# ScalarE sets one bank of a group's first maxima aside; VectorE takes its maximum later

## The chip, the cores and the metric

The kernel runs on one core of a Trainium2 chip. The metric is the device time of one launch in microseconds (us), taken as the median over runs. The core has five engines that work beside each other, each through its own queue in order: TensorE (PE in the profile, with its weight loads as PEld), VectorE (DVE), ScalarE (ACT), GpSimd (POOL) and SyncE (SP), which here only issues DMA transfers. Matmul results land in eight accumulation banks (PSUM), each 128 partitions by 512 fp32 numbers; all other tiles lie in on-chip memory (SBUF). Engines wait for each other on semaphores only.

## The reference

One pre-norm decoder layer on x of shape (2, 2048, 512) in fp32. The change touches its first part, self-attention with 16 heads of 64 and a relative-position bias:

```python
x = x + _L0_attn_ref(_layernorm(x), Wq, Wk, Wv, Wo, rel_bias)
    # q, k, v = proj(Wq), proj(Wk), proj(Wv)
    # scores = einsum('bhqd,bhkd->bhqk', q, k) + bias[buckets]
    # attn   = softmax(scores, axis=-1)
    # ctx    = einsum('bhqk,bhkd->bhqd', attn, v) @ Wo.T
x = x + _L0_xattn_ref(_layernorm(x), ctx_1024, ...)   # cross-attention, 77 keys
x = x + _L0_ffn_ref(_layernorm(x), ...)               # routed feed-forward
```

The softmax needs, for each query, a number near the maximum of its scores, so that no exponential overflows. The kernel calls it the guard.

## The kernel before, in words

The program has three stages, `attention`, `middle` and `routed`. Attention treats 32 heads (2 batch rows times 16) one after the other. A head has two query blocks of 1024 queries and, for each, 16 key tiles of 128 keys: 32 **steps**, two to a **group**, 16 groups a head. Heads overlap: while head n is scored, the guard maxima of head n+1 are taken (from group 3 on; groups 0 to 2 finish those of head n) and the projection of head n+2 runs.

What one group g of the steady state does, in the order in which each queue is written:

- **TensorE**: `largest(g, 0)` (lines 602 to 619), two matmuls that write 128 queries by 512 keys into each of the banks 6 and 7; `scores` of steps 2g and 2g+1 (621 to 638), six matmuls each into two banks, with two more guard matmuls (633) in the first two key tiles of a query block; `largest(g, 1)`, the same for the next 512 keys, into the same banks 6 and 7; in groups 2, 6, 10, 14 a quarter of a projection (583 to 600), 12 matmuls into bank 5; `value` of steps 2g-2 and 2g-1 (640 to 651), eight matmul instructions in all; in groups 9 and 1 `sum_of` (653 to 659), which waits for GpSimd's accumulated probabilities.
- **VectorE**: `largest(g, 0)` (939 to 947), one maximum over both banks, 1024 numbers per partition; `near` (956 to 964), the bias of the near diagonal for those steps that have one (18 of 32, steps 0 to 8 and 23 to 31); `largest(g, 1)`; then, by group, `step` (972, groups 3, 7, 11, 15), `step_lo` (979, groups 4, 8, 12, 0), `queries_low` (966, groups 2, 6, 10, 14), `guards` (949, groups 2 and 10), `reciprocals`.
- **ScalarE**: `exp` of steps 2g and 2g+1 (810 to 826) into a ring of four buffers `probs`; then by group `step_hi`, `take_out` and `keys_out` (copies of bank 5), `values_out`, `sums_out`; in group 0 first `split_w`.
- **GpSimd**: for each step one addition of `probs` into the accumulator `acc` (lines 351 and 354), 30 a head, each waiting on the one before; twice a head `context` (325 to 329), once a head the low part of a weight (335).

The waits that tie these together: `largest` on TensorE may write banks 6 and 7 only when VectorE has reduced what they held (semaphore `max_done`, lines 610 to 613); `scores` of a step waits for the `exp` two steps earlier, whose banks it takes; `exp` of a step waits for its scores, for `near` if it has one, and for the `value` and the GpSimd addition of the step four earlier (the ring). SyncE loads each head's keys and queries into `stacks` (407 to 425); `largest` in group 3 is the first to wait for them (607 to 609).

`largest` of VectorE in one line, which the change takes apart:

```python
dve.tensor_reduce(maxes[:, qt:qt + HALF_GROUPS // 2 + 1:HALF_GROUPS // 2, first_chunk + pair],
                  ps[:, bank:bank + 2, :], AX.X, ALU.max).then_inc(s["max_done"], 1)
```

Of the kernel before, what the change touches and what calls it, by code (L numbers as in the profile page):

```python
# [10 lines left out]
ALU = mybir.AluOpType  # L11
ACT = mybir.ActivationFunctionType
AX = mybir.AxisListType


P = 128
# [14 lines left out]
GROUPS = STEPS // 2  # L31
HALF_GROUPS = GROUPS // QBLK
# [111 lines left out]
def max_turn(g):  # L144

    if g <= LAST_MAX:
        return 0, GROUPS - 1 - LAST_MAX + g
    return 1, g - FIRST_MAX


def max_tiles(turn):

    half, pair = divmod(turn // 2, HALF_GROUPS // 2)
    return half * NT // 2 + pair, 2 * (turn % 2)
# [12 lines left out]
def attention(nc, io, scr, homes):  # L167

    with ExitStack() as c:
        def sb(name, shape, dt=F32):  # L170
            return c.enter_context(nc.sbuf_tensor(name, shape, dt))
# [30 lines left out]
        ident = sb("ident", [P, P])  # L202
        ones = sb("ones", [P, DK])
        maxes = sb("maxes", [P, NT, CHUNKS])
        neg_max = sb("neg_max", [P, NT], F32R)
        part = sb("part", [P, PART])
        part_inv = sb("part_inv", [P, PART])
# [14 lines left out]
        ps = c.enter_context(nc.psum_tensor("ps", [P, 8, 512], F32))  # L222
# [19 lines left out]
        def max_bank(n, pair):  # L242

            early = isinstance(n, int) and n < 0
            return (MX, SC)[pair] if early else MX

        def value_bank(v):
# [3 lines left out]
        names = """const_ready consts_in bias_max bias_table bias_mm bias_stored wv_hi wv_lo stat  # L251
            moment rstd1 rstd2 xn turned xhi xlo vps vout w_in w_hi w_split
            proj q_hi k_own k_hi q_lo step step_hi step_lo fill_q fill_k fill_d
            maxed max_done neg_ready neg_stored neg_in
            scored biased exped summed pved summ sum_out spread recip recip_stored recip_in
            ctx_raw ctx near_tab held ctx_stored zeros lead kv_in wo_in wq2_in rows_in
            k2_zero k2mm k2 v2mm v2 wo_hi wo_lo last_summ last_recip last_ctx""".split()
# [16 lines left out]
        def past(engine, name, value):  # L274

            if not isinstance(value, int) or value > 0:
                engine.wait_ge(name, value)
# [21 lines left out]
        def has_max(n, g):  # L299

            _, own, nxt, _ = parts(n)
            return own if g <= LAST_MAX else nxt
# [243 lines left out]
        def _(pe):  # L546
# [55 lines left out]
            def largest(n, side, g, pair):  # L602

                late, turn = max_turn(g)
                m, mside = (n + 1, 1 - side) if late else (n, side)
                qt, first_chunk = max_tiles(turn)
                if late and g == FIRST_MAX and pair == 0:
                    pe.wait_ge(s["fill_q"], FILLS_Q * (m + 1))
                    pe.wait_ge(s["fill_k"], FILLS_K * (m + 1))
                if isinstance(n, int) and n < 0:  # L610
                    past(pe, s["max_done"], 2 * turn + pair - 1)
                else:
                    past(pe, s["max_done"], GROUPS * 2 * m + 2 * turn + pair)
                q = slice((qt // 8 * 4 + qt % 8) * P, (qt // 8 * 4 + qt % 8 + 1) * P)
                keys = slice((first_chunk + pair) * 512, (first_chunk + pair + 1) * 512)
                for half in range(2):
                    mm = pe.matmul(ps[:, max_bank(n, pair) + half, :], stacks[lane(half), mside, QS, q], stacks[lane(half), mside, KH[half], keys],  # L617
                                   start=True, stop=True)
                mm.then_inc(s["maxed"], 1)
# [125 lines left out]
        def _(act):  # L745
# [45 lines left out]
            def step_hi(m, tb):  # L791
# [3 lines left out]
                    past(act, s["fill_d"], FILLS_D * m)  # L795
                act.copy(c_d[0:64, LOOKBACK + tb * 512:LOOKBACK + (tb + 1) * 512].bitcast(F32R), ps[0:64, proj_bank(m, tb), :]).then_inc(s["step_hi"], 1)

            def sums_out(n, qb):

                act.wait_ge(s["summ"], 2 * n + qb + 1)  # L800
                past(act, s["ctx"], 2 * n + qb)
                act.copy(sums[:, 0:QUARTER], ps[:, PB, 0:QUARTER]).then_inc(s["sum_out"], 1)
# [48 lines left out]
            def head(n, k, side):  # L851
                carry, own, nxt, prep = parts(n)
                if isinstance(n, int) and n == -2:
                    first_head()
                    return
                if isinstance(n, int) and n == 0:
                    for q in range(V_RING):
                        act.wait_ge(s["vstored"][q], 16 * 2 * NT // V_RING)
                for g in range(GROUPS):
                    if g == 0 and prep:  # L860
                        split_w(n + 2)
                    if own:
                        exp(n, k, side, 2 * g)
                        exp(n, k, side, 2 * g + 1)
                    if prep and g in STEP_GROUPS:
                        step_hi(n + 2, STEP_GROUPS[g])
                    if prep and g in EVAC_GROUPS:
                        take_out(n + 2, EVAC_GROUPS[g])
                        keys_out(n + 2, EVAC_GROUPS[g])
                    if g == 0 and carry:  # L870
                        values_out(n - 1, 1)
                    if g == HALF_GROUPS and own:
                        values_out(n, 0)
                    if isinstance(n, int) and n == -1:
                        for v in halves_of_group(g):
                            vout(v)
                    if g in SUM_GROUPS:
                        qb = SUM_GROUPS[g]
                        if own if qb == 0 else carry:
                            sums_out(n if qb == 0 else n - 1, qb)  # L880
# [8 lines left out]
        def _(dve):  # L889
# [49 lines left out]
            def largest(n, side, g, pair):  # L939

                late, turn = max_turn(g)
                m = n + 1 if late else n
                at = GROUPS * 2 * m + 2 * turn + pair
                dve.wait_ge(s["maxed"], at + 1)
                bank = max_bank(n, pair)
                qt, first_chunk = max_tiles(turn)
                dve.tensor_reduce(maxes[:, qt:qt + HALF_GROUPS // 2 + 1:HALF_GROUPS // 2, first_chunk + pair], ps[:, bank:bank + 2, :], AX.X, ALU.max).then_inc(s["max_done"], 1)  # L947

            def guards(m, half):

                q = slice(half * 8, half * 8 + 8)
                dve.wait_ge(s["max_done"], GROUPS * 2 * m + GROUPS * (half + 1))
                past(dve, s["neg_stored"], 16 * (2 * m + half - 1))
                dve.tensor_reduce(neg_max[:, q], maxes[:, q, :], AX.X, ALU.max, negate=True).then_inc(s["neg_ready"], 1)

# [77 lines left out]
            def head(n, k, side):  # L1033
                carry, own, nxt, prep = parts(n)
                if isinstance(n, int) and n == -2:
                    first_head()
                    return
                for g in range(GROUPS):
                    lowered = None
                    if g in LOW_GROUPS:  # L1040
                        tb = LOW_GROUPS[g]
                        if tb < BLOCKS - 1 and prep:
                            lowered = (n + 2, tb)
                        if tb == BLOCKS - 1 and own and nxt:
                            lowered = (n + 1, tb)
                    if has_max(n, g):
                        largest(n, side, g, 0)
                    if own:
                        near(n, k, side, 2 * g)
                        near(n, k, side, 2 * g + 1)  # L1050
                    if has_max(n, g):
                        largest(n, side, g, 1)
                    if prep and g in STEP_GROUPS:
                        step(n + 2, STEP_GROUPS[g])
                    if lowered:
                        step_lo(*lowered)
                    if prep and g in EVAC_GROUPS:
                        queries_low(n + 2, EVAC_GROUPS[g])
                    if isinstance(n, int) and n == NH - 1:
                        if g == KEYS_GROUP - 1:  # L1060
                            dve.wait_ge(s["scored"], (NH - 1) * STEPS)
                            dve.memset(k2[:], 0.0).then_inc(s["k2_zero"], 1)
                        if g == KEYS_GROUP:
                            keys_out(0)
                        if g == VALUES_GROUP:
                            key_values_out(0)
                    if g == FIRST_MAX + NT // 2 - 1 and nxt:
                        guards(n + 1, 0)
                    if g == LAST_MAX and own:
                        guards(n, 1)  # L1070
                    if g in RECIP_GROUPS:
                        qb = RECIP_GROUPS[g]
                        if own if qb == 0 else carry:
                            reciprocals(n if qb == 0 else n - 1, qb)
# [1367 lines left out]
```

## Time and profile before

| what | value |
|---|---|
| median of 3 runs | 3798.07 us (3797.63 to 3800.9) |
| the profiled execution, its own time | 3797.64 us |
| its span in the trace | 3795.8 us |
| mean granted TensorE clock | 0.989 of 2.4 GHz |
| busy: TensorE, VectorE, ScalarE, GpSimd | 97%, 65%, 53%, 71% of the span |

The busy shares are means over three stages. Attention's steady part, from about 300 to 2650 us, is where the change acts. A line of a timeline gives start, duration from the first start to the last end of a run of equal instructions, engine, line, operation, tiles, shape and count; brackets hold the idle time of the engine just before and what ended it. Ends of matmuls are modelled, so their starts are the better guide. In rows that group instructions by line the numbers behind the bar are busy time, mean of one in ns, and idle time of the engine before them with what ended it.

### The profile page before, as it was taken

The numbers are of one execution on the slowest core, as the hardware profiler recorded it, in microseconds if no ns is written. First come the engines' busy times: TensorE is split into PE (matmuls) and PEld (weight loads), VectorE is DVE, ScalarE is ACT, GpSimd is POOL, SyncE is SP. The second block draws the span as 40 slices with busy tenths as digits, with TensorE's granted clock in tenths as the row PEclk, the third lists the DMA queues.
The fourth block names the chain that finished last, engine by engine and source line by source line (L and its number), as shares of the span: only waits on it lengthen the run. The fifth ranks groups of instructions, "written<-read, shape, count | busy, mean of one in ns | idle before, by whom it ended". The sixth has DMA issues, their size and how long they took to land. (4 is left out here: it accounts for less than half of the span.)

```text
span 3795.8 us, 62609 instructions
## 1 busy us (share of the span) xinstructions
PE 3681.4 (97%) x21277; PEld 2195.6 (58%) x21277; DVE 2450.3 (65%) x3356; ACT 2016.1 (53%) x3452; POOL 2684.2 (71%) x1402
## 2 busy tenths in 40 slices
PE   9989999999999999999999999999979999997899
PEld 7755545555555555554555555555438888884387
DVE  3456676666666766776667776677526777774731
ACT  3336566666666665666666665666534555553232
POOL 1119999999999999999999999999963434430010
PEclk9989999999999999999999999999989999998999
DMA  7662223432234352243223333233322333335710
GB/s 222 160 145 64 70 70 82 103 76 69 70 74 106 100 139 70 70 106 83 72 68 71 99 89 72 67 72 89 92 79 76 104 97 106 105 125 197 248 37 23
DMA packets 368346, 366.60 MB, mean 97 GB/s; under 512 B 189339, under 2 KB 261531, under 8 KB 362776
## 3 DMA queue, kind: packets, MB, share of 16 engines
q1 hardware_dynamic: 299064, 336.50, 32.9%
q10 hardware_dynamic: 67168, 20.98, 2.4%
q0 software_dynamic: 1920, 6.29, 0.5%
q8 instruction: 151, 2.47, 0.3%
q14 instruction: 43, 0.35, 0.0%
HBM read 142.64 MB, written 89.70 MB: 61 GB/s over the span
## 5 line engine op out<-in xcount | busy, mean ns | idle before, releaser
L354 POOL TENSOR_TENSOR acc<-acc,probs 128x1024 f32<-128x1024 f32 x894 | 2131.8, 2385 | 147.0 <-ACT probs L822 35.5
L947 DVE TENSOR_REDUCE maxes<-ps 128x2 f32<-128x1024 f32 x1024 | 1251.3, 1223 | 474.2 <-PE ps L617 462.2
L825 ACT ACTIVATE probs<-ps,far_bias 128x1024 f32<-128x1024 f32 (+7 forms) x1280 | 999.0, 819 | 722.2 <-DVE near_s L964 447.1
L648 PE MATMUL ps<-probs,v_head 128*64 128x512 f32 x4096 | 993.7, 606 | 0.4 <-ACT probs L822 0.4
L636 PE MATMUL ps<-stacks 64*128 64x512 f32 x6144 | 810.9, 392 | 6.1 <-ACT probs L822 5.3
L636 PEld LDWEIGHTS ps<-stacks 64*128 64x128 f32 x6144 | 579.9, 186 | 133.3 <-ACT probs L822 12.6
L617 PE MATMUL ps<-stacks 64*128 64x512 f32 x2048 | 504.1, 490 | 17.5 <-DVE maxes L947 12.2
L617 PEld LDWEIGHTS ps<-stacks 64*128 64x128 f32 x2048 | 191.5, 184 | 565.1 <-DVE maxes L947 424.2
L648 PEld LDWEIGHTS ps<-probs,v_head 128*64 128x64 f32 x4096 | 248.6, 136 | 443.2 <-issue 441.8
L964 DVE TENSOR_TENSOR near_s<-ps,near_bias 128x384 f32<-128x384 f32 (+2 forms) x576 | 265.0, 491 | 37.2 <-PE ps L636 34.3
L970 DVE TENSOR_TENSOR c_q<-ps,c_q 64x512 fp32r<-64x512 f32 x128 | 87.5, 684 | 306.6 <-ACT c_q L781 306.6
L822 ACT ACTIVATE probs<-near_s 128x384 f32<-128x384 f32 (+2 forms) x576 | 273.4, 475 | 0.0
L597 PE MATMUL ps<-xn_hi,w_hi 128*128 128x512 f32 x512 | 216.0, 422 | 0.0
L597 PE MATMUL ps<-xn_lo,w_hi 128*128 128x512 f32 x512 | 203.0, 396 | 0.0
L597 PE MATMUL ps<-xn_hi,w_lo 128*128 128x512 f32 x512 | 202.8, 396 | 0.0
L1291 POOL TENSOR_TENSOR m_rs<-m_rs,m_expo 128x1 f32<-128x1 f32 x32 | 17.6, 550 | 234.1 <-DVE m_rs L1535 234.1
L573 PE MATMUL ps<-stacks,xn_hi 128*128 128x512 f32 x512 | 164.4, 403 | 10.6 <-DVE xn_lo L916 8.5
L781 ACT CAST c_q<-ps 64x512 fp32r<-64x512 f32 x128 | 74.1, 579 | 177.5 <-PE ps L597 177.5
L351 POOL TENSOR_TENSOR acc<-probs 128x1024 f32<-128x1024 f32 x64 | 151.7, 2370 | 3.2 <-ACT probs L822 3.2
L1439 ACT COPY m_pt<-m_ps 77x512 f32<-77x512 f32 x128 | 68.4, 582 | 106.0 <-PE m_ps L1322 106.0
L1426 PEld LDWEIGHTS m_ps<-m_turned,both_wk 128*128 128x128 f32 x1024 | 121.9, 196 | 4.5 <-ACT m_turned L1484 2.0
L597 PEld LDWEIGHTS ps<-xn_hi,w_hi 128*128 128x128 f32 x512 | 96.5, 188 | 47.9 <-issue 30.5
(278 smaller groups left out, 4557.6 us busy)
## 6 DMA issues: line engine op xcount, KB each, us to landing
stacks<-c_q SPq DMA_DIRECT2D x128, 256.0 KB, 4.3
stacks<-c_d SPq DMA_DIRECT2D x64, 512.0 KB, 6.9
stacks<-c_k SPq DMA_DIRECT2D x32, 768.0 KB, 5.6
stacks<-c_k SPq DMA_DIRECT2D x64, 384.0 KB, 7.2
scr_v<-probs ACTq DMA_DIRECT2D x32, 512.0 KB, 4.1
v_head<-scr_v SPq DMA_DIRECT2D x32, 512.0 KB, 3.7
scr_ctx<-ctx_out SPq DMA_DIRECT2D x128, 128.0 KB, 2.3
both_ctx<-scr_ctx SPq DMA_DIRECT2D x32, 512.0 KB, 3.9
```

Source lines behind the costliest of these rows:

```text
L351: pool.tensor_tensor(acc[:, qb, :], probs[:, (st - 1) % PT_RING, :], pr, ALU.add).then_inc(s["summed"], 2)
L354: pool.tensor_tensor(acc[:, qb, :], acc[:, qb, :], pr, ALU.add).then_inc(s["summed"], 1)
L573: mm = pe.matmul(ps[:, value_bank(v), :], xs[i][:, k, t * P:(t + 1) * P], (wv_hi, wv_lo)[j][:, k, half * 512:(half + 1) * 512], start=at = ...
L597: mm = pe.matmul(ps[:, proj_bank(m, tb), :], w[wi][:, kk, :], xs[xi][:, kk, tb * 512:(tb + 1) * 512], start=a == 0, stop=a == len(TERMS) - 1)
L617: mm = pe.matmul(ps[:, max_bank(n, pair) + half, :], stacks[lane(half), mside, QS, q], stacks[lane(half), mside, KH[half], keys], start=Tr ...
L636: mm = pe.matmul(ps[:, bank + half, :], stacks[lane(half), side, of_keys[half], keys], stacks[lane(half), side, QS, of_queries], start=Fal ...
L648: mm = pe.matmul(ps[64 * half:64 * half + 64, PV, :], v_head[:, side, kt, :], probs[:, st % PT_RING, half * 512:(half + 1) * 512], start=k ...
L822: ins = act.activation(probs[:, st % PT_RING, a:z], near_s[:, st % 2, 0:z - a], ACT.Exp)
L825: ins = act.activation(probs[:, st % PT_RING, a:z], sc[:, a:z], ACT.Exp, bias=bias)
L947: dve.tensor_reduce(maxes[:, qt:qt + HALF_GROUPS // 2 + 1:HALF_GROUPS // 2, first_chunk + pair], ps[:, bank:bank + 2, :], AX.X, ALU.max).t ...
L964: dve.tensor_tensor(near_s[:, st % 2, 0:z - a], sc, near_bias[:, side, j0:j0 + z - a], ALU.add).then_inc(s["biased"], 1)
L1426: mm = pe.matmul(ps[:, Q2, m * P:(m + 1) * P], wq2[:, k, m * P:(m + 1) * P], turned1[:, k, :], start=k == 0, stop=k == KT - 1)
```

## The change

Of the two banks that `largest(g, 0)` fills, VectorE reduces only the first at once (512 numbers instead of 1024). ScalarE copies the second into a new tile `aside` (128 x 512 fp32) at the head of its group, ahead of the two exponentials. After its reduction of the second pair, VectorE reduces that copy. TensorE's second pair waits for both the first reduction and the copy; its first pair waits for the copy of the group before. The second pair's own reduction stays whole.

```diff
+        aside = sb("aside", [P, 512])
...
 TensorE, largest
+                if pair == 0:
+                    past(pe, s["aside"], GROUPS * m + turn)
+                elif not (isinstance(n, int) and n < 0):
+                    past(pe, s["aside"], GROUPS * m + turn + 1)
...
 ScalarE
+            def set_aside(n, g):
+                late, turn = max_turn(g)
+                m = n + 1 if late else n
+                act.wait_ge(s["maxed"], GROUPS * 2 * m + 2 * turn + 1)
+                past(act, s["aside_done"], GROUPS * m + turn)
+                act.copy(aside[:], ps[:, max_bank(n, 0) + 1, :]).then_inc(s["aside"], 1)
...
                 for g in range(GROUPS):
+                    if has_max(n, g):
+                        set_aside(n, g)
                     if g == 0 and prep:
                         split_w(n + 2)
...
 VectorE, largest
-                dve.tensor_reduce(maxes[:, qt:qt + HALF_GROUPS // 2 + 1:HALF_GROUPS // 2, first_chunk + pair], ps[:, bank:bank + 2, :], AX.X, ALU.max).then_inc(s["max_done"], 1)
+                if pair == 0:
+                    dve.tensor_reduce(maxes[:, qt:qt + 1, first_chunk], ps[:, bank, :].unsqueeze(1), AX.X, ALU.max).then_inc(s["max_done"], 1)
+                else:
+                    dve.tensor_reduce(maxes[:, qt:qt + HALF_GROUPS // 2 + 1:HALF_GROUPS // 2, first_chunk + 1], ps[:, bank:bank + 2, :], AX.X, ALU.max).then_inc(s["max_done"], 1)
+            def largest_aside(n, g):
+                late, turn = max_turn(g)
+                m = n + 1 if late else n
+                qt, first_chunk = max_tiles(turn)
+                dve.wait_ge(s["aside"], GROUPS * m + turn + 1)
+                dve.tensor_reduce(maxes[:, qt + HALF_GROUPS // 2:qt + HALF_GROUPS // 2 + 1, first_chunk], aside[:].unsqueeze(1), AX.X, ALU.max).then_inc(s["aside_done"], 1)
...
 guards
+                dve.wait_ge(s["aside_done"], GROUPS * m + HALF_GROUPS * (half + 1))
...
                     if has_max(n, g):
                         largest(n, side, g, 1)
+                        largest_aside(n, g)
                     if prep and g in STEP_GROUPS:
                         step(n + 2, STEP_GROUPS[g])
```

## Rows read from the trace of the kernel before

**Rows 1.** Stage table: stretch, PE, PEld, DVE, ACT, POOL busy, clock, DMA, GB/s

```profile
1500.00:2000.00 500.00, 500.00 (x2872) 253.27 (x2872) 346.84 (x416) 302.32 (x492) 472.14 (x208) 1.00 0.32 77
```

**Rows 2.** Timeline of GpSimd: the first addition of two successive heads

```profile
1542.17 2.37 POOL L351 TENSOR_TENSOR acc<-probs 128x1024 f32<-128x1024 f32 x1
...
1621.68 2.38 POOL L351 TENSOR_TENSOR acc<-probs 128x1024 f32<-128x1024 f32 x1
```

**Rows 3.** Groups by line, GpSimd, one head (1542.25 to 1621.65): its additions

```profile
L354 POOL TENSOR_TENSOR acc<-acc,probs 128x1024 f32<-128x1024 f32 x28 | 66.8, 2385 | 4.4 <-ACT probs L822 1.0
```

**Rows 4.** Waits of the whole run, GpSimd: us in total, times, longest

```profile
POOL acc L354 <- ACT probs L822: 35.5, 62, 1.8
```

**Rows 5.** Timeline of one group with a bound second pair, 1516.5 to 1520.8

```profile
1516.51 0.58 ACT L796 CAST c_d<-ps 64x512 fp32r<-64x512 f32 x1 [0.91 <-DVE ps L977]
1516.61 1.55 PE L636 MATMUL ps<-stacks 64*128 64x512 f32 x12
1516.81 1.23 DVE L947 TENSOR_REDUCE maxes<-ps 128x2 f32<-128x1024 f32 x1 [0.33 <-PE ps L617]
...
1518.09 0.49 PE L617 MATMUL ps<-stacks 64*128 64x512 f32 x2
1518.51 0.20 PEld L648 LDWEIGHTS ps<-probs,v_head 128*64 128x64 f32 x4 [0.24 <-issue]
...
1520.12 0.69 DVE L983 TENSOR_TENSOR c_k<-ps,c_d 64x512 fp32r<-64x512 f32 x1
```

**Rows 6.** Timeline of a group with guard matmuls, end of its scores, 1537.2 to 1538.3

```profile
1537.22 0.86 PE L636 MATMUL ps<-stacks 64*128 64x512 f32 x6
...
1537.91 0.39 PE L617 MATMUL ps<-stacks 64*128 64x512 f32 x2
...
1538.23 1.94 PE L648 MATMUL ps<-probs,v_head 128*64 128x512 f32 x8
```

**Rows 7.** Timeline of group 3 of a head up to GpSimd's step 6

```profile
1552.24 1.54 PE L636 MATMUL ps<-stacks 64*128 64x512 f32 x12
1552.44 1.23 DVE L947 TENSOR_REDUCE maxes<-ps 128x2 f32<-128x1024 f32 x1 [0.71 <-PE ps L617]
1553.59 0.88 DVE L964 TENSOR_TENSOR near_s<-ps,near_bias 128x384 f32<-128x384 f32 x2
...
1555.45 7.44 POOL L354 TENSOR_TENSOR acc<-acc,probs 128x1024 f32<-128x1024 f32 x3 [0.75 <-ACT probs L822]
```

**Rows 8.** Timeline of group 9's end: the sum on TensorE and GpSimd's next addition

```profile
1583.99 0.64 PE L658 MATMUL ps<-acc,ones 128*32 128x256 f32 x8
1584.09 2.38 POOL L354 TENSOR_TENSOR acc<-acc,probs 128x1024 f32<-128x1024 f32 x1
```

**Rows 9.** Groups by line, head 1542.2 to 1621.7: sizes of like instructions

```profile
L947 DVE TENSOR_REDUCE maxes<-ps 128x2 f32<-128x1024 f32 x32 | 39.1, 1223 | 14.5 <-PE ps L617 14.1
...
L970 DVE TENSOR_TENSOR c_q<-ps,c_q 64x512 fp32r<-64x512 f32 x4 | 2.7, 684 | 9.1 <-ACT c_q L781 9.1
...
L808 ACT COPY ctx_out<-ps 128x512 f32<-128x512 f32 x2 | 1.2, 587 | 1.0 <-PE ps L648 1.0
```

**Rows 10.** Timeline of the middle stage: VectorE reduces from on-chip memory beside GpSimd

```profile
2917.50 1.43 DVE L1595 TENSOR_REDUCE m_sm<-m_e 128x16 f32<-128x1232 f32 x1
2917.66 0.55 POOL L1291 TENSOR_TENSOR m_rs<-m_rs,m_expo 128x1 f32<-128x1 f32 x1 [7.19 <-DVE m_rs L1535]
```

**Rows 11.** Line 617 of TensorE: idle before it, us and times

```profile
  DMA stacks<-c_k: 3.7, 2
```

**Rows 12.** Timeline of two long waits of TensorE, 2664 and 2734

```profile
2664.92 0.80 PE L617 MATMUL ps<-stacks 64*128 64x512 f32 x2 [2.51 <-DMA stacks<-c_k]
...
2734.19 0.64 PE L658 MATMUL ps<-acc,ones 128*32 128x256 f32 x8 [0.99 <-POOL acc L354]
```

**Rows 13.** Stage table, the stretches behind those two waits (columns as in rows 1)

```profile
2664.70:2668.20 3.50, 3.28 (x16) 2.69 (x16) 1.78 (x2) 0.49 (x1) 2.38 (x2) 0.51 0.48 117
...
2733.00:2736.00 3.00, 2.01 (x20) 1.22 (x20) 0.70 (x1) 1.62 (x4) 3.00 (x2) 1.00 0.00 0
```

More of the change, by code:

```diff
@@ L253, in attention @@
             proj q_hi k_own k_hi q_lo step step_hi step_lo fill_q fill_k fill_d
-            maxed max_done neg_ready neg_stored neg_in
+            maxed max_done aside aside_done neg_ready neg_stored neg_in
             scored biased exped summed pved summ sum_out spread recip recip_stored recip_in
```

## The prediction

> **What bounds the kernel now.** I read the stage table first. In attention's steady part TensorE is busy all of 500 us and GpSimd 472 of them [rows 1]. Two engines are near the end of their time, and the question is which of them a saving on the other runs into.
>
> The second view is GpSimd's own. Successive heads begin 1621.68 - 1542.17 = 79.51 us apart [rows 2]. Within a head 28 additions of 2385 ns have 4.4 us of idle time before them, of which only 1.0 us is a wait for ScalarE [rows 3]. The other 3.4 us are spread over the 24 additions that directly follow another: 0.14 us each, the price of an addition that waits for the one before. No faster TensorE takes that away. The 1.0 us falls on two additions, which would have paid 0.14 each anyway. So GpSimd really waits 1.0 - 0.28 = 0.72 us a head, and its floor is 79.51 - 0.72 = 78.8 us a head. **GpSimd stands 0.9% below the present pace**, and that caps this change.
>
> The third view is the timeline of TensorE in one group. Where guard matmuls make the scores longer, the second pair is on time: three pairs of score matmuls begin at 1537.22, the second pair of maxima at 1537.91, so 0.23 us a pair, and the values follow 0.32 us later [rows 6]. In an ordinary group six pairs begin at 1516.61, and the maxima are due 6 x 0.23 = 1.38 later, at 1517.99. They begin at 1518.09, 0.05 us behind the end of VectorE's reduction (1516.81 + 1.23 = 1518.04), and the values follow after 0.42 instead of 0.32 [rows 5]. That is 0.10 us late and 0.10 us more behind it, since a weight load that has to wait isn't hidden: **0.20 us lost**, none of it shown as idle time. The written order gives 14 such groups a head (all but groups 0 and 8, which have guard matmuls): 2.8 us, 3.5% of a head.
>
> **The change, part by part.**
> - *The first reduction is halved.* The whole one takes 1223 ns for 1024 numbers; a half costs at least 612 (half of it), and at most 721, if the 1232 numbers at 1427 [rows 10] against 1024 at 1223 give 0.98 ns a number and the rest is fixed [rows 9, 10]. I take 0.68, the nearest row with 512 numbers from a bank (684) [rows 9]. In rows 5's group it would end at 1517.49, half a microsecond before the pair is due at 1517.99.
> - *The copy.* ScalarE copies 128 x 512 out of a bank in 587 ns [rows 9]; a head gets 16 of them, 9.4 us, and ScalarE is busy 302 of 500 us [rows 1]. It hides in the time in which ScalarE waits for the scores behind the pair. Rows 5 show a bad case: ScalarE works on another copy until 1517.09. The copy then ends at 1517.68 and with 0.05 for the signal at 1517.73, still ahead of 1517.99. If that cover is gone, each tenth of a microsecond of lateness costs TensorE a tenth, up to the old 0.20.
> - *The late reduction.* Another 0.68 us on VectorE, behind the second pair's. With the halved first one that makes 0.68 + 0.68 - 1.22 = 0.14 us more a group, 2.2 a head; VectorE is idle 30% [rows 1]. Queued behind it are step, step_lo and queries_low. A step_lo of 0.69 us [rows 5] ends some groups, and with 0.68 ahead of it the next first reduction begins about as much later as it got shorter. So the four groups behind a step_lo collect nothing, and ten groups x 0.20 = 2.0 us a head remain for TensorE.
> - *Reading the copy beside GpSimd.* The new reduction reads on-chip memory while GpSimd adds there. At worst GpSimd would stand still for all of it, 16 x 0.68 = 10.9 us a head, and at best it notices nothing. In the middle stage a reduction of the same kind runs from 2917.50 to 2918.93, and a GpSimd operation that begins inside it at 2917.66 is done 0.55 us later [rows 10]: it wasn't held until the reduction's end. That excludes the worst case, and I take nothing.
> - *The added waits.* TensorE gets one more per pair, 32 a head. Below nothing isn't possible; above, 0.05 us each (the signal delay in rows 5), 1.6 a head. I take nothing, because most signals arrive long before; the cover is the surplus of 2.0 - 0.72 us found below. The guards' new wait directly follows the reduction that it waits for: nothing.
> - *Step_lo of group 0 comes 0.68 us later*, and SyncE's last loads of keys wait for it. TensorE asks for them in group 3, and twice in the run it waited there, 3.7 us in all [rows 11]. With loads later and TensorE earlier more heads will meet it, for some tenths. I put this against the hiccups that a TensorE with surplus absorbs: nothing in sum.
>
> **What GpSimd lets through.** Its one large wait is at step 6, in group 3: 0.75 us, 0.61 beyond the usual gap [rows 7]. There the halved reduction helps a second time. The bias addition of step 6 began at 1553.59 only because the reduction ran until 1553.67; the scores were streamed by 1552.24 + 0.69, plus a matmul's tail of 0.16 (0.39 [rows 6] less 0.23), 1553.09, and the half reduction ends at 1553.12. So step 6 comes about 0.44 us sooner from this alone. Ahead of it, TensorE passes groups 10 to 15 and 1 to 2 of which two follow a step_lo: six x 0.20 = 1.2 us. Together 1.6 against 0.61 needed. Hence GpSimd's waits all but vanish, and **GpSimd sets the pace**.
>
> The surplus goes into a new wait. In group 9 TensorE sums what GpSimd has accumulated; today it starts that at 1583.99, just as GpSimd turns to its next addition at 1584.09 [rows 8], a tie. A faster TensorE waits there, for up to 2.0 - 0.72 = 1.3 us a head.
>
> **The sum.** 29 steady heads x 0.72 = 20.9 us. The whole run allows 35.5 - 62 x 0.14 = 26.8 us of such waits at most [rows 4]; the first and last heads, which wait for loads, hold the rest, and I count none of it. The profiled execution took 3797.64 us, 0.43 below the median of 3798.07; 3797.64 - 20.9 = 3776.7, and I say **3777** for either.
>
> The clock speaks against this. After TensorE had waited 2.51 us for a load [rows 12], the granted clock in the 3.5 us behind it was 0.51, the lower of its levels, 1.2 GHz; after a wait of 0.99 us it stayed at 1.00 (2.4 GHz) [rows 12, 13]. The new wait of 1.3 us is nearer to the second, so the sum has no clock term. [...]
>
> **Rivals.**
> - *The wait only changes hands.* TensorE's second pair now needs two engines, and the later one counts. If the copy usually stands behind a late exponential, or the late reduction pushes the next first one back in most groups, TensorE keeps its pace and so does GpSimd: 3790 to 3801. Rows 5 speak against it (both in time even in a busy group); for it, VectorE gets more work per group, not less.
> - *The clock drops once a head.* Place: the sum in group 9. A stretch of 3.5 us at half the clock loses 1.75 us of matmuls, on the very path from there to the next head's step 6 that gained 1.6 and needs 0.61. It would end 1.75 - 1.6 = 0.15 us longer than now at least, and 0.55 if the 0.44 of VectorE doesn't come: 29 x 0.55 = 16, 3813. It decides once the wait nears 2.5 us, or if lower ones suffice. **Slower.**
> - *GpSimd's floor isn't one.* If its recorded spans are stretched and it could go faster when fed, TensorE's whole 2.8 us a head would come: 29 x 2.8 = 81, 3716. Against it stand the 24 gaps of 0.14 us, which GpSimd pays although its input is there [rows 3].
>
> **How the numbers follow.** A measurement here tells about 0.2% (7.6 us) from no change. Forecast (GpSimd's floor, 3769 to 3788): 0.76. Wait changes hands: 0.13, counted as the same. Clock and any other loss: 0.07, slower. No floor: 0.04, faster. So faster 0.80, same 0.13, slower 0.07. The low end 3769 is all of rows 4's 26.8 and a little from the first heads; the high end 3794 takes half of the case without change.
>
> **What would show it.** Right: heads begin 78.8 us apart; the additions' idle time per head falls from 4.4 to about 3.8 without a wait for ScalarE; the second pair follows its scores by 0.23; TensorE idles ahead of the sums of group 9; ScalarE's waits for GpSimd grow. Wrong: a copy that ends behind the scores in most groups, additions longer than 2385 ns, a granted clock below 1 within heads, or heads still 79.5 us apart though the second pair is on time.

## The result and the profile after

The changed kernel takes **3843.72 us** (median of four, 3841.22 to 3850.07) against 3797.85 for the kernel before: ratio 1.012, 95% interval 1.0108 to 1.0133. It is 46 us slower, where 3777 was forecast, and it lies outside the range. Lines have moved: `largest` of TensorE is L622, scores L641, values L653; VectorE's two first reductions are L963 (half, first pair) and L965 (whole, second pair), the late one L973; ScalarE's copy is L809, `split_w` L778, the exponentials L835 and L838; GpSimd adds at L352 and L355.

The page of the profile after, two of its parts: busy time by engine, and a row of the table of DMA queues (packets, MB, share).

```profile
span 3839.4 us, 65841 instructions
...
PE 3648.9 (95%) x21277; PEld 2210.0 (58%) x21277; DVE 2510.8 (65%) x3868; ACT 2290.1 (60%) x3964; POOL 2684.2 (70%) x1402
...
q14 instruction: 124, 1.02, 0.1%
```

TensorE, at 97% before, is at 95%; ScalarE rose from 53% to 60% by the copies. A row to remember: queue 14, which brings instructions, moved 124 packets, where the kernel before had 43.

GpSimd's timeline, the first addition of a head's first query block, as in [rows 2]:

```profile
1566.63 2.41 POOL L352 TENSOR_TENSOR acc<-probs 128x1024 f32<-128x1024 f32 x1
...
1646.95 2.35 POOL L352 TENSOR_TENSOR acc<-probs 128x1024 f32<-128x1024 f32 x1 [1.09 <-ACT probs L835]
...
1729.96 2.37 POOL L352 TENSOR_TENSOR acc<-probs 128x1024 f32<-128x1024 f32 x1
```

Heads are 80.3 and 83.0 us apart, not 79.51 and not the 78.8 forecast, and the bracket, a wait for ScalarE, stands in every second head. The list of waits says who is late (total us, times, longest):

```profile
PE ps L622 <- ACT aside L809: 72.2, 45, 5.0
...
ACT aside L809 <- issue: 61.6, 13, 5.1
```

TensorE's second pair waits for the copy, 72.2 us in all, and the copy waits 13 times, 4.7 us each, for "issue": for nothing that the profile shows. One of the 13, in the timeline of all engines:

```profile
1638.04 0.69 DVE L963 TENSOR_REDUCE maxes<-ps 128x1 f32<-128x512 f32 x1
1638.04 0.58 ACT L801 CAST c_d<-ps 64x512 fp32r<-64x512 f32 x1 [0.71 <-DVE ps L1004]
...
1643.42 0.58 ACT L809 COPY aside<-ps 128x512 f32<-128x512 f32 x1 [4.80 <-issue]
1643.91 0.62 ACT L778 CAST w_hi<-w_in 128x512 fp32r<-128x512 f32 x1
...
1644.15 0.80 PE L622 MATMUL ps<-stacks 64*128 64x512 f32 x2 [4.69 <-ACT aside L809]
...
1644.88 3.68 PE L653 MATMUL ps<-probs,v_head 128*64 128x512 f32 x8
```

The copy's input was there by 1638.04, when VectorE began to reduce the other bank of the pair (L963); both wait for the same signal of the pair's matmuls, and the late reduction of the group before had ended at 1637.28. ScalarE has ended its last instruction of a head at 1638.62 and does nothing until 1643.42. The copy is the first instruction of a head. The eight value matmuls behind it take 3.68 us, where they took 1.94 in [rows 6]; the stage table (columns as in [rows 1]) tells why:

```profile
1500.00:2000.00 500.00, 482.73 (x2802) 250.56 (x2800) 351.58 (x505) 349.33 (x582) 460.38 (x203) 0.98 0.32 77
1638.00:1643.00 5.00, 1.46 (x14) 0.84 (x10) 1.68 (x4) 0.58 (x1) 4.71 (x3) 1.00 1.03 279
1643.40:1646.80 3.40, 2.65 (x8) 1.01 (x10) 1.81 (x2) 3.31 (x6) 2.08 (x2) 0.50 1.03 228
1646.80:1650.20 3.40, 3.40 (x14) 1.49 (x12) 1.38 (x3) 1.17 (x2) 2.35 (x1) 0.50 0.55 160
```

Behind TensorE's wait of 4.69 us the granted clock is 0.50 (1.2 GHz) in both stretches shown, 6.8 us. Elsewhere the change does what was forecast, as in this group (the counterpart of [rows 5]):

```profile
1575.20 0.50 PE L622 MATMUL ps<-stacks 64*128 64x512 f32 x2
...
1575.54 1.54 PE L641 MATMUL ps<-stacks 64*128 64x512 f32 x12
1575.75 0.69 DVE L963 TENSOR_REDUCE maxes<-ps 128x1 f32<-128x512 f32 x1 [0.71 <-PE ps L622]
1575.82 0.59 ACT L809 COPY aside<-ps 128x512 f32<-128x512 f32 x1 [0.51 <-PE ps L622]
...
1576.92 0.39 PE L622 MATMUL ps<-stacks 64*128 64x512 f32 x2
...
1577.24 0.20 PEld L653 LDWEIGHTS ps<-probs,v_head 128*64 128x64 f32 x4 [0.35 <-issue]
```

Copy and half reduction are over by 1576.44, the second pair comes 1576.92 - 1575.54 = 1.38 us behind its scores, exactly the time of six pairs, and the values 0.32 later. So the loss that the views show sits in one place, at the start of every second head.

### The profile page after: what moved, and what is told of

Read it like the earlier page. It is cut to its first block and busy times, and to the rows that moved or that the text cites. A ratio compares the mean times of both kernels' runs of the same rounds, so it can differ in the third digit from the quotient of the medians.

```text
span 3839.4 us, 65841 instructions
## 1 busy us (share of the span) xinstructions
PE 3648.9 (95%) x21277; PEld 2210.0 (58%) x21277; DVE 2510.8 (65%) x3868; ACT 2290.1 (60%) x3964; POOL 2684.2 (70%) x1402
## 3 DMA queue, kind: packets, MB, share of 16 engines
q14 instruction: 124, 1.02, 0.1%
## 5 line engine op out<-in xcount | busy, mean ns | idle before, releaser
L355 POOL TENSOR_TENSOR acc<-acc,probs 128x1024 f32<-128x1024 f32 x894 | 2131.6, 2384 | 172.2 <-ACT probs L835 55.7
L838 ACT ACTIVATE probs<-ps,far_bias 128x1024 f32<-128x1024 f32 (+7 forms) x1280 | 999.8, 818 | 200.9 <-DVE near_s L991 118.8
L653 PE MATMUL ps<-probs,v_head 128*64 128x512 f32 x4096 | 1015.6, 617 | 0.5 <-ACT probs L835 0.5
L641 PE MATMUL ps<-stacks 64*128 64x512 f32 x6144 | 814.4, 393 | 10.3 <-ACT probs L835 5.8
L965 DVE TENSOR_REDUCE maxes<-ps 128x2 f32<-128x1024 f32 x512 | 625.5, 1222 | 254.5 <-PE ps L622 252.4
L641 PEld LDWEIGHTS ps<-stacks 64*128 64x128 f32 x6144 | 583.5, 186 | 138.0 <-ACT probs L835 12.9
L622 PE MATMUL ps<-stacks 64*128 64x512 f32 x2048 | 477.3, 462 | 89.4 <-ACT aside L809 72.2
L653 PEld LDWEIGHTS ps<-probs,v_head 128*64 128x64 f32 x4096 | 252.6, 138 | 466.4 <-issue 464.9
L622 PEld LDWEIGHTS ps<-stacks 64*128 64x128 f32 x2048 | 198.0, 186 | 552.6 <-DVE maxes L965 246.7
L963 DVE TENSOR_REDUCE maxes<-ps 128x1 f32<-128x512 f32 x512 | 352.6, 689 | 230.2 <-PE ps L622 223.7
L809 ACT COPY aside<-ps 128x512 f32<-128x512 f32 x512 | 299.9, 586 | 230.5 <-PE ps L622 157.2
L973 DVE TENSOR_REDUCE maxes<-aside 128x1 f32<-128x512 f32 x512 | 346.2, 676 | 2.7 <-ACT aside L809 1.7
L991 DVE TENSOR_TENSOR near_s<-ps,near_bias 128x384 f32<-128x384 f32 (+2 forms) x576 | 283.0, 497 | 79.1 <-PE ps L641 57.0
L835 ACT ACTIVATE probs<-near_s 128x384 f32<-128x384 f32 (+2 forms) x576 | 273.6, 475 | 0.0
L352 POOL TENSOR_TENSOR acc<-probs 128x1024 f32<-128x1024 f32 x64 | 151.8, 2373 | 15.1 <-ACT probs L835 15.1
```

The lines of the kernel that those rows point to most:

```text
L355: pool.tensor_tensor(acc[:, qb, :], acc[:, qb, :], pr, ALU.add).then_inc(s["summed"], 1)
L641: mm = pe.matmul(ps[:, bank + half, :], stacks[lane(half), side, of_keys[half], keys], stacks[lane(half), side, QS, of_queries], start=Fal ...
L653: mm = pe.matmul(ps[64 * half:64 * half + 64, PV, :], v_head[:, side, kt, :], probs[:, st % PT_RING, half * 512:(half + 1) * 512], start=k ...
L809: act.copy(aside[:], ps[:, max_bank(n, 0) + 1, :]).then_inc(s["aside"], 1)
L835: ins = act.activation(probs[:, st % PT_RING, a:z], near_s[:, st % 2, 0:z - a], ACT.Exp)
L838: ins = act.activation(probs[:, st % PT_RING, a:z], sc[:, a:z], ACT.Exp, bias=bias)
```

## The experiments

What begins there? ScalarE's program isn't written out head by head. A helper puts the steady heads into a loop of two a pass:

```python
head(-2, -1, 0)
head(-1, -1, 1)
head(0, 0, 0)
with engine.Fori(0, NH // 2 - 2) as j:
    head(j * 2 + 1, j, 1)
    head(j * 2 + 2, j + 1, 0)
for n in range(NH - 3, NH):
    head(n, n // 2, n % 2)
```

With 32 heads it runs 14 times and branches back 13 times, as often as ScalarE stalls; behind the 14th branch, which isn't taken, there is no such wait. Counted in the records of the trace, waits included, a pass of ScalarE had 363 instructions before and has 440 after. (VectorE's grew from 241 to 309 and shows no such wait, nor does GpSimd's of 200; TensorE's program is written out.) And in ScalarE's idle time above, from 1638.62 to 1643.42, the instruction queue is at work:

```profile
q14 instruction: 2, 0.02, 1.5%
```

Such a packet starts inside each of the 13 waits; in the kernel before, none does within 4 us behind any of its 13 taken branches. **Theory F**: at the branch, ScalarE waits for its own code to be fetched. **Rival C**: the place of the copy, first in the head and ahead of its first exponentials, makes ScalarE late.

**1. The loop written out**, in the changed kernel and, as a control, in the one before:

```diff
-            heads(act, head)
+            for n in range(-2, NH):
+                head(n, n // 2, n % 2)
```

> The change, with ScalarE's loop over pairs of heads written out head by head (no branch); work and order are those of the changed kernel. Theory F (code fetch: ScalarE's loop grew from 363 to 440 recorded instructions a pass, and at the end of each pass it stands still for about 4.8 us until its code is there again): the 4.8 us waits of TensorE in group 0 of every second head are gone, heads stand about 78.8 us apart and the time is about 3777 us. Rival C (place of the copy: TensorE's second pair waits for a copy that ScalarE reaches late, wherever its code lies): stays near 3844 us.

> The kernel before, with ScalarE's loop written out in the same way: the control for the first run. Theory F: no stall was there to remove, 3798 us within 0.2%. Rival C: 3798 us too. If it is faster by 10 us or more, the writing out itself brings something, and the first run has to be read against this one.

Measured: the change without the loop takes **3774.12 us** (ratio 0.9935, 0.9919 to 0.9952), the control 3799.48 (1.0005, 0.9995 to 1.0014). The copy is still first in its head, so C falls; F stands. The work on the tiles and its order are the same in both versions of the change. Writing out also drops the loop's register arithmetic (in the records, two heads of the change take about 328 instructions instead of 440, of the control about 265 instead of 363); the control shows that this alone brings nothing. So the loop costs 3843.72 - 3774.12 = 69.6 us, 5.35 a branch. The stalls are 61.6 us of ScalarE's time, and behind them TensorE ran slower: in the trace some 80 us of attention's steady part stand at a granted clock of 0.50, which would be up to 40 us of lost matmul time. The two together are more than 69.6, so part of them is absorbed; how much of each isn't separated. This version beats both kernels. Its GpSimd timeline, a line of its groups in one head (1568.9 to 1647.6, as [rows 3]) and two of its waits:

```profile
1489.93 2.36 POOL L352 TENSOR_TENSOR acc<-probs 128x1024 f32<-128x1024 f32 x1
...
1568.82 2.38 POOL L352 TENSOR_TENSOR acc<-probs 128x1024 f32<-128x1024 f32 x1
...
1647.67 2.38 POOL L352 TENSOR_TENSOR acc<-probs 128x1024 f32<-128x1024 f32 x1
```

```profile
L355 POOL TENSOR_TENSOR acc<-acc,probs 128x1024 f32<-128x1024 f32 x28 | 66.8, 2385 | 3.7
```

```profile
ACT probs L838 <- POOL acc L355: 161.7, 180, 2.4
...
PE ps L622 <- ACT aside L809: 15.2, 35, 2.0
...
PE ps L663 <- POOL acc L355: 7.6, 16, 0.6
```

Heads are 78.89 and 78.85 us apart, GpSimd's additions have 3.7 us of idle time a head and no wait for ScalarE in it.

**2. Only a longer loop**, in the kernel before: three waits (long fulfilled) in each group of ScalarE, and one.

```diff
                 for g in range(GROUPS):
+                    for _ in range(3):
+                        act.wait_ge(s["wv_hi"], 1)
```

> The kernel before, with three waits on a semaphore that has long been reached added to each group of ScalarE: about 363 + 96 = 459 instructions a pass of its loop, and no copy, no other work. Theory F: a stall of about 4.8 us at the end of each of 14 passes, as in the changed kernel; 3820 to 3860 us. Rival C: 3798 us, since ScalarE has time for 3 short waits a group.

> As the run before, with one such wait a group: about 395 instructions a pass. Theory F: 3798 us if the room for a loop lies above 395, some 3820 to 3860 us if it lies between 363 and 395; it places the edge. Rival C: 3798 us.

Measured: 3833.66 (ratio 1.0094, 1.0077 to 1.0111) and 3831.11 (1.0088, 1.0072 to 1.0105). ScalarE's first copy of a pass waits 13 times for "issue", a line from the list of waits of each run:

```profile
ACT w_hi L773 <- issue: 49.8, 13, 3.9
```

```profile
ACT w_hi L773 <- issue: 48.7, 13, 3.8
```

So waits without any work, and without any copy, bring the stall into the kernel before. But two waits can share an instruction: by the records the passes have 396 and 364 instructions, not 459 and 395, and 364 is only one more than 363. A limit of length exactly there would be a coincidence. The heads ahead of the loop hold the waits too, and so in the second run the loop begins 16 instructions further on in the code. Two readings follow: **A**, the loop must lie well on the blocks in which the code is fetched; **L**, its length alone decides.

**3. Only a shift.** The same waits once, ahead of the loop, at the start of ScalarE's program. Two waits make one instruction: 180 of them move the loop by 90, 90 by 45 (both in the changed kernel), 48 by 24 (in the kernel before).

```diff
         def _(act):
+            for _ in range(48):
+                act.wait_ge(s["consts_in"], 48)
             act.wait_ge(s["bias_mm"], 1)
```

> The changed kernel, loop and all, with 180 waits that have long been reached at the very start of ScalarE's program, which make 90 instructions: ScalarE's loop (440 instructions) lies 90 instructions later in its code and nothing else is changed. Theory A (alignment: the code comes in fixed blocks, of 256 instructions by the Trainium skill, Runtime: NRT & Kernel Launch, section Instruction fetch mechanics, and a loop is free of stalls if it lies within two of them): the loop now fits into two blocks, no stall, about 3774 us as with the loop written out. Theory L (length: a loop of over 363 instructions is fetched again): 3844 us.

> As the run before, with half the filler: the loop lies 45 instructions later and begins, by the estimate, still ahead of a block's edge, so that it touches three blocks. Theory A: the stall stays, about 3844 us. Theory L: 3844 us. If this run is at 3774 us as well, the filler itself cures, or the blocks lie otherwise than thought.

> The kernel before, its loop of 363 instructions as it is, with 24 filler instructions at the start of ScalarE's program. Theory A: the loop's end is pushed into a third block, a stall of about 3.8 us in each of 13 passes as in the run with one wait a group: about 3831 us. Theory L: 3798 us.

Measured: the changed kernel 3830.79 (ratio 1.0078, 1.0061 to 1.0095) shifted by 90 and 3878.05 (1.0205, 1.0188 to 1.0222) by 45; the kernel before, shifted by 24, 3829.99 (1.008, 1.0063 to 1.0097). **Twenty-four instructions that do nothing, run once, cost 31 us.** The shift by 90 shortens the stall from 4.7 to 3.6 us (46.7 in 13) but doesn't remove it, though by the placing found in experiment 5 the 440 instructions would there lie in two blocks of 256: A falls in this form, as L falls by the shift of 24. With 45 there are two a pass, the second at the first exponential: the 11th record behind the branch comes over 5 us after the 10th in all 13 passes (the list of waits puts nine of these down to "issue"). Two lines of that list, and ScalarE's timeline:

```profile
ACT aside L811 <- issue: 46.8, 13, 3.7
ACT probs L840 <- issue: 44.9, 9, 5.8
```

```profile
1492.05 0.58 ACT L803 CAST c_d<-ps 64x512 fp32r<-64x512 f32 x1 [0.70 <-DVE ps L1006]
1496.15 0.58 ACT L811 COPY aside<-ps 128x512 f32<-128x512 f32 x1 [3.52 <-issue]
1496.63 0.62 ACT L780 CAST w_hi<-w_in 128x512 fp32r<-128x512 f32 x1
1501.98 0.90 ACT L840 ACTIVATE probs<-ps,far_bias 128x768 f32<-128x768 f32 x1 [4.73 <-issue]
```

**4. Which shifts are good?** The kernel before with 256, 512 and 384 such waits: shifts of 128, 256 and 192 instructions. A packet of queue 14 is 1.02 MB / 124 = 8.2 KB; if that is 128 instructions, the pattern should repeat with 128. The control of experiment 1 supports the 128: its code up to the next stage's loop has 3444 recorded instructions more than that of the kernel before, and it moved 70 packets instead of 43, so 3444 / 27 = 128 each.

> The kernel before with 256 waits on a semaphore that has long been there (two are put into one instruction, so 128 instructions) at the start of ScalarE's program; the loop itself is unchanged, 363 recorded instructions a pass. With 24 instructions there the loop stalled 3.8 us at its branch and the time was 3829.99. If only the loop's place among blocks of 128 instructions (8 KB, the size of one packet of instructions) decides, the loop stands as in the kernel before: no stall, 3799 to 3803 us (the idle instructions themselves cost at most some 4 us at the start). If the blocks are of 256 instructions, or any code ahead of the loop is enough, it stalls as with 24: 3.8 us in 13 passes, 3828 to 3835.

> The same with 512 waits, 256 instructions. If the loop's place among blocks decides, of 128 or of 256 instructions, the loop stands again as in the kernel before: no stall, 3799 to 3810 us (with up to 10 us for the idle instructions themselves at the start). If code ahead of the loop is enough whatever its length, 3.8 us in 13 passes: 3830 to 3840 us.

> The kernel before with 384 such waits, 192 instructions, ahead of ScalarE's loop. So far the same loop stalled with 24 instructions ahead and not with 0, 128 or 256. If its place within blocks of 128 instructions decides (192 is 64 beyond the last place that was good), it stalls again: 3.6 to 3.9 us in 13 passes, some 48 us of ScalarE's time in all; 3840 to 3850 us, of which some 11 us are the idle instructions at the start. If two blocks of 256 instructions have to hold it, a stretch of good places lies between 128 and 256, 192 is in it, and there is no stall: 3806 to 3812 us.

Measured: 3804.08 (ratio 1.0012, 1.0003 to 1.0022), 3813.93 (1.0039, 1.0025 to 1.0054) and 3843.32 (1.0113, 1.0084 to 1.0143). ScalarE's waits for "issue" of 10 us and more in the three, one fence each:

```profile
ACT L750 <- issue: 13.5, 1, 13.5
```

```profile
ACT L750 <- issue: 23.5, 1, 23.5
```

```profile
ACT w_hi L775 <- issue: 48.0, 13, 3.8
...
ACT L750 <- issue: 18.7, 1, 18.7
```

The waits at L750, once, are the idle instructions themselves, and they explain the small losses of the first two. The 13 stalls come back only with 192. So good places repeat every 128 instructions. This is the branch in ScalarE's timeline with a shift of 24, and then with 128:

```profile
1472.44 0.58 ACT L798 CAST c_d<-ps 64x512 fp32r<-64x512 f32 x1
1476.58 0.62 ACT L775 CAST w_hi<-w_in 128x512 fp32r<-128x512 f32 x1 [3.56 <-issue]
```

```profile
1464.95 0.58 ACT L798 CAST c_d<-ps 64x512 fp32r<-64x512 f32 x1
1465.44 0.62 ACT L775 CAST w_hi<-w_in 128x512 fp32r<-128x512 f32 x1
```

**5. Where the edge is.** The reading that experiments 3 and 4 suggest: code comes in blocks of 128 instructions, and a loop that lies within three of them (384) is not fetched again. If the second stall above, 11 behind the branch, marks an edge (to within one instruction), the loops can be placed: that kernel's starts 11 short of an edge, 117 behind the one ahead of it. Counted in the records, it starts 102 instructions later than the loop of the kernel before (45 by the shift, 57 by the change), which so starts 117 - 102 = 15 behind an edge and ends at 15 + 363 = 378, six short of 384. So a shift of 4 should be free and one of 9 not.

> The kernel before with 8 waits, 4 instructions, ahead of ScalarE's loop. The reading so far: code comes in blocks of 128 instructions, and a pass is free of fetches when the loop lies within three of them (384 instructions). The kernel with two stalls a pass had its second one 11 instructions behind the branch; if a block's edge is there, the loop of the kernel before (363 instructions) starts 15 behind an edge and ends 6 short of the third block's end. With 4 instructions ahead it then still fits: no stall, 3797 to 3803 us. If a few instructions ahead are enough, whatever the edges, it stalls: 3.6 to 3.9 us in 13 passes, 3826 to 3834 us.

> The same with 18 waits, 9 instructions. If the loop has to lie within three blocks of 128 and ended 6 short of an edge, it now reaches 3 beyond it: it stalls 3.6 to 3.9 us in 13 passes, 3826 to 3834 us. If the edges lie otherwise (so far only that 17 to 24 instructions are too many is known), there is no stall: 3797 to 3803 us.

Measured: **3800.4** (ratio 0.9996, 0.9986 to 1.0005) with 4, **3826.39** (1.0075, 1.0058 to 1.0091) with 9. Each page's row of queue 14, and the wait of the second:

```profile
q14 instruction: 43, 0.35, 0.0%
```

```profile
q14 instruction: 108, 0.88, 0.1%
```

```profile
ACT w_hi L775 <- issue: 46.1, 13, 3.8
```

43 packets as in the kernel before, then 108. The reading predicted both, from an edge found in another kernel. The edge itself is shown only to lie between 4 and 9 instructions behind the loop's old end. And 440 instructions are more than 384, so by it the changed kernel has no good place for its loop; the three places measured (0, 45, 90) all stalled. A loop of the change shortened to under 384 wasn't tried.

The Trainium skill (Runtime: NRT & Kernel Launch, section Instruction fetch mechanics) states that a taken branch whose target is outside the present window of code has to fetch it before execution goes on; the 13 stalls for 13 branches agree. It puts the window at two blocks of 256 instructions. That would make 128 and 192 alike, and the runs don't show it: period 128, and three blocks hold. Why three is not shown. One thing in the records bears on it: in the trace with the shift of 9, (108 - 43) / 13 = 5 packets are fetched a pass, though the 363 instructions lie in four blocks. If one block is always fetched ahead, a loop of three and that one make four blocks held; no run tests this.

## Why the prediction was wrong

- **The step that failed** is the copy's cost: "It hides in the time in which ScalarE waits for the scores behind the pair." The copy's *time* does hide; 16 x 588 ns a head are still there in the version without the loop, which is faster than before. What was left out is its *code*: 32 copies and their waits made ScalarE's pass 77 instructions longer, and the room for a looped engine's code was a term that the sum put at nothing without naming it. The bound given there, "up to the old 0.20" of lateness, missed 13 waits of 4.7 us, since the list of bounds held only work that the trace of before shows. That trace shows no stall: by the reading of experiment 5 its loop fitted with about six instructions to spare.
- **The clock rival** was half right. Behind a wait of 4.69 us the granted clock was 0.50, as it was 0.51 behind one of 2.51 in [rows 12, 13]. But the wait is that for code, at group 0 of every second head, not for the sums in group 9, so that neither its place nor its price (3813) came out. The waits for the sums did come in the run without the loop, 16 times and at most 0.6 us, and its mean granted clock between 300 and 2650 us is 1.00.
- **GpSimd's floor of 78.8 us a head was right**: 78.85 to 78.89 without the loop, idle time 3.7 against the 3.8 expected, no wait for ScalarE, and 3774.12 against 3777. The case that GpSimd has no floor falls, and so does the one that the wait only changes hands: a head is 0.6 us shorter. All this is the version without the loop; the forecast was for the one with it.
- **The sizes**: half reduction 689 ns (0.68 taken), late reduction 676 (0.68), copy 586 (587), GpSimd's additions 2384 as before [rows 3], so the read of the copy beside it cost nothing. The second pair follows its scores by 1.38 us, as worked out.
- **The surplus** of TensorE was expected as waits ahead of the sums in group 9, up to 1.3 us a head. These are 7.6 us in the run without the loop, 16 times. TensorE is idle 30.5 us between 300 and 2650 us there (1.6 before), about 1.0 us a head. The largest waits are now ScalarE's, 161.7 us for GpSimd's additions (40.7 in the kernel before). TensorE's 15.2 us of waits for the copy fit with that, since the copy stands in ScalarE's queue behind the late exponentials; no run separates it.

## What to carry to other kernels

An engine whose program is a loop pays for added instructions twice: in their time, which the trace of before can price, and in the loop's code, which it can't. Count the instructions of a pass, waits included, before an edit adds to it, and read two rows afterwards: waits for "issue" at the first instruction of a pass, and the packets of the instruction queue. Here, on ScalarE, a loop within three blocks of 128 ran free; a longer one, or the same one a few instructions further on, lost 3.5 to 5 us of that engine's time at each branch, and writing the loop out took the loss away. Other engines' loops weren't tried.

## What was not expected of the hardware

Nine idle instructions at the start of one engine's program cost 25 us (3826.39 against 3801.15 for the kernel before beside it), four cost nothing. The same change is 46 us slower or 25 us faster (3774.12 against 3798.93) with the same work on the tiles in the same order, by how ScalarE's heads are written. A loop's place alone moved the changed kernel between 3830.79 and 3878.05. VectorE's loop, also longer (309 instructions, still under 384), shows no stall in the changed kernel.
